# Cached keys of the paged attention turned ahead of time on VectorE and kept in DRAM, in place of TensorE transposes

## The reference

```python
q = rmsnorm(x @ Wq.T) ; k = rmsnorm(x @ Wk.T) ; v = x @ Wv.T   # 32, 8, 8 heads of 128
q, k = rope(q, pos), rope(k, pos)                    # pos = cache_seqlens + token
kc = k_cache[block_table].reshape(bsz, 512, 8, 128)  # 16 pages of 32 tokens
vc = v_cache[block_table].reshape(bsz, 512, 8, 128)
k_all, v_all = concat(kc, k), concat(vc, v)          # 640 keys
scores = where(valid, q . k_all * SCALE, -1e30)      # valid: token < cache_seqlens
o = softmax(scores) . v_all
attention2 = o.reshape(b, s, 32 * 128) @ Wo.T
x = x + attention_0(...) ; x = x + ffn_0(...)
x = x + attention_1(...) ; x = x + quantised_ffn(attention2)
```

## Time and profile before

| | us |
|---|---|
| median of 3 runs | 2040.61 (2037.54 to 2041.23) |
| the profiled execution, whole | 2036.61 |
| its span in the trace | 2034.7 |
| PE busy | 1986.8, 98% |
| DVE busy | 1534.6, 75% |
| ACT busy | 1324.8, 65% |
| POOL busy | 805.8, 40% |

### The profile page before, as it was taken

One profiled execution on the slowest core, in us unless ns is written; L12 is line 12 of the kernel. 1 busy time (PEld: TensorE's weight loads), 2 busy tenths in 40 slices (PEclk: granted clock), 3 DMA queues, 4 the chain that ended last, 5 costly groups with the idle time before them and its releaser, 6 DMA issues.

```text
span 2034.7 us, 35876 instructions
## 1 busy us (share of the span) xinstructions
PE 1986.8 (98%) x12477; PEld 1695.1 (83%) x12477; DVE 1534.6 (75%) x3383; ACT 1324.8 (65%) x3796; POOL 805.8 (40%) x797
## 2 busy tenths in 40 slices
PE   6999999999999999999999999999999999999997
PEld 5778677888888888888888888888888888888774
DVE  6777764556656555687887888878878888888998
ACT  4676763445554544576776777767767767777785
POOL 3200015100000000056666666666666666666662
PEclk9999999999999999999999999999999999999999
DMA  7301101101201110121111111211211111112010
GB/s 261 99 28 48 53 1 73 62 32 37 68 32 39 56 53 1 58 79 31 62 53 31 63 51 32 71 44 36 80 32 63 53 32 62 53 31 83 26 31 37
DMA packets 45011, 108.62 MB, mean 53 GB/s; under 512 B 15634, under 2 KB 21010, under 8 KB 40354
## 3 DMA queue, kind: packets, MB, share of 16 engines
q1 hardware_dynamic: 28450, 72.74, 10.3%
q0 software_dynamic: 16384, 33.59, 5.6%
HBM read 103.14 MB, written 3.15 MB: 52 GB/s over the span
## 4 chain that ended last, share of the span: by engine, by line
PE 91%; DVE 4%; ACT 3%; issue 1%; DMA 1%; SPq 0%; DVEq 0%; ACTq 0%
PE PS L1662 10%; PE PS L1487 9%; PE PS L1430 9%; PE PS L1566 9%; PE PS L1674 8%; PE PS L1629 7%; PE PS L1647 7%; PE PS L1580 4%; PE PS L1443 4%; PE PS L1632 3%; PE PS L342 3%; PE PS L1458 3%; PE PS L1473 2%; PE PS L498 1%; PE PS L1465 1%; PE PS L1598 1%
## 5 line engine op out<-in xcount | busy, mean ns | idle before, releaser
L2528 POOL DMA_INDIRECT kcache<-in_kcache,rows x256 | 249.6, 975 | 533.1 <-DVE x_res L1829 462.4
L2536 POOL DMA_INDIRECT vcache<-in_vcache,rows x256 | 257.2, 1005 | 124.2 <-issue 58.4
L2002 DVE CUSTOM_DVE_ANT_0 pr<-PS,ffn_weights,sm 128x640 f32<-128x640 f32 x256 | 224.6, 885 | 87.5 <-PE PS L1632 87.5
L2387 ACT ACTIVATE pr<-pr,sm 128x640 f32<-128x640 f32 x256 | 212.5, 830 | 40.1 <-DVE sm L2002 39.3
L2018 DVE TENSOR_TENSOR prT_lo<-PS,prT_hi 128x512 fp32r<-128x512 f32 x320 | 209.2, 686 | 37.0 <-ACT prT_hi L2398 30.8
L2398 ACT ACTIVATE prT_hi<-PS 128x512 fp32r<-128x512 f32 x320 | 178.0, 597 | 61.1 <-PE PS L1647 60.5
L1647 PE MATMUL PS<-consts,pr 128*128 128x128 f32 x1280 | 172.3, 273 | 2.2 <-DVE prT_lo L2018 1.7
L1647 PEld LDWEIGHTS PS<-consts,pr 128*128 128x128 f32 x1280 | 149.7, 141 | 26.3 <-DVE prT_lo L2018 2.7
L2542 POOL TENSOR_TENSOR vcached_lo<-vcache,vcached_hi 128x512 fp32r<-128x512 f32 x64 | 83.7, 1308 | 218.7 <-ACT vcached_hi L2370 218.7
L1629 PE MATMUL PS<-kT_hi,qT_hi 128*128 128x320 f32 x512 | 154.4, 309 | 2.5 <-DVE sm L2002 1.2
L1629 PE MATMUL PS<-kT_lo,qT_hi 128*128 128x320 f32 x512 | 154.1, 309 | 0.0
(11 more groups left out here) (321 smaller groups left out, 6178.1 us busy)
## 6 DMA issues: line engine op xcount, KB each, us to landing
arena<-in_wqkv SPq DMA_DIRECT2D x16, 1536.0 KB, 6.5
arena<-in_wo SPq DMA_DIRECT2D x16, 1024.0 KB, 5.4
arena<-in_wcT SPq DMA_DIRECT2D x8, 1024.0 KB, 6.7
kcache<-in_kcache,rows POOLq DMA_INDIRECT x256
vcache<-in_vcache,rows POOLq DMA_INDIRECT x256
arena<-in_xT SPq DMA_DIRECT2D x8, 256.0 KB, 7.8
x_res<-in_x SPq DMA_DIRECT2D x1, 2048.0 KB, 13.5
ffn_weights<-in_alibi SPq DMA_DIRECT2D x2, 1024.0 KB, 7.1
```

The source lines that it names most:

```text
L2002: dve.tensor_tensor_reduce(pr2[:, h, :].rearrange("p (a n) -> p a n", a=2), PS[:, SCORE_BANK[h]:SCORE_BANK[h] + 2, 0:HALF], keymask[:, b, ...
L2387: act.activation(pr2[:, h, :], pr2[:, h, :], ACT.Exp, bias=nm2[:, h:h + 1], scale=-1.0, accum_out=rs2[:, h:h + 1]).then_inc(a2_ex, 1)
L2528: pool.indirect_dma_start(out=kcache[:, c, :], out_offset=None, in_=T["kcache"], in_offset=bass.IndirectOffsetOnAxis(ap=rows[:, g, b, c:c ...
L2536: pool.indirect_dma_start(out=vcache[:, c, :], out_offset=None, in_=T["vcache"], in_offset=bass.IndirectOffsetOnAxis(ap=rows[:, g, b, c:c ...
```

## The change

- PE's turn_cached_k is gone. The keys are turned during attention 1 by DVE: POOL gathers the keys of item n (four gathers of 128 rows) in another order of rows into key_pages, DVE transposes them in blocks of 32x32 (turn_keys, one instruction of 128x512 float32), and POOL stores the result (256 KB, rows of 512 bytes) to a DRAM tensor turned_kept. The 64 turns are done at the end of DVE's step1(i) for i = 5 to 61: one in an item, two when i % 8 is 5.
- The row numbers of these gathers come from key_page_i, loaded at the start by four more transfers of SP. Each of them spreads 32 page numbers, which lie 4 elements apart in DRAM, over 32 partitions, so its elements are 4 bytes each.
- In attention 2 SP loads the turned keys of an item by four transfers of 64 KB into kcache; ACT's hi_of_cached_k and DVE's lo_of_cached_k read kcache instead of bank 3. SP waits for the last store before the first of these loads. The weight loads are put between them, at b = 2.
- pool_masks now waits for the last of the 64 stores, since the masks lie where the key buffers were. Then come load_values(0) and factors(0), as before. POOL issues no key loads in attention 2.
- project_out(i) goes to bank 3 (the last item's to bank 0) and waits for two of the four row maxima; the wait for add(i-1) in scores moves from head 0 to head 1.
- Order: DVE does lo_of_o(i-1) before the row maxima, reciprocals(2, 3) before normalise(1), lo_of_cached_k after add. ACT does normalise(2) and (3) before k_squares and hi_of_own_v, and hi_of_cached_k after hi_of_probs(1); for item 0 it stands in item 62 of attention 1, ahead of kT_copy1(63).

The diff, cut:

```diff
             for q in range(4):
                 sp.dma_start(page_i[q * 32:(q + 1) * 32, :], T["pages"][q, :].partition_broadcast(32)).then_inc(s_setup, 16)
+            for q in range(4):
+                sp.dma_start(key_page_i[q * 32:(q + 1) * 32, :],
+                             T["pages"].rearrange("c (b q) -> q (c b)", q=CHUNKS)[q, :].partition_broadcast(32),
+                             allow_slow_non_contiguous=True).then_inc(s_setup, 16)
...
+            dve.tensor_scalar(key_row0[:], key_page_i[:], float(PAGE * G), cst["inpage"],
+                              ALU.mult, ALU.add).then_inc(s_setup, 1)
...
+        key_pages = fw[:, B * D:B * D + 2 * CACHED].rearrange("p (s c d) -> p s c d", s=2, c=CHUNKS)
+        key_turned = fw[:, B * D + 2 * CACHED:B * D + 4 * CACHED].rearrange("p (s r c n) -> p s r c n", s=2, r=4, c=CHUNKS)
+        key_rows = area(28160, G * B * CHUNKS).bitcast(I32).rearrange("p (g c b) -> p g c b", g=G, c=CHUNKS)
+        turned_kept = nc.dram_tensor("turned_keys", [ITEMS, 4, P, P], F32).ap()
+        FIRST_TURN, LAST_TURN = GH + 1, ITEMS - 3
+
+        def turns_in(i):
+            if not FIRST_TURN <= i <= LAST_TURN:
+                return range(0)
+            first = i - FIRST_TURN + (i - FIRST_TURN + B - 1) // B
+            return range(first, min(first + 1 + (i % B == FIRST_TURN), ITEMS))
+
+        def pool_turned_keys(pool):
+            def gather(n):
+                g, b = group_of(n)
+                wait(pool, s_kpt, n - 1)
+                wait(pool, s_kpg, 16 * CHUNKS * n)
+                for c in range(CHUNKS):
+                    pool.indirect_dma_start(out=key_pages[:, n % 2, c, :], out_offset=None, in_=T["kcache"],
+                                            in_offset=bass.IndirectOffsetOnAxis(ap=key_rows[:, g, c, b:b + 1], axis=0)
+                                            ).then_inc(s_kpg, 16)
+
+            def store(n):
+                pool.wait_ge(s_kpt, n + 1)
+                wait(pool, s_kps, 16 * n)
+                pool.dma_start(turned_kept[n, :, :, :].rearrange("r p n -> p r n"),
+                               key_turned[:, n % 2, :, :, :].rearrange("p r c n -> p r (c n)")).then_inc(s_kps, 16)
+
+            pool.wait_ge(s_x2, B)
+            ch = Chain(pool, s_chp, counted["pool"])
+            ch.link(pool.tensor_tensor(key_rows.rearrange("p g c b -> p g (c b)"),
+                                       key_row0[:].unsqueeze(1).broadcast_to([P, G, B * CHUNKS]),
+                                       kvhead[:].unsqueeze(2).broadcast_to([P, G, B * CHUNKS]), ALU.add))
+            counted["pool"] = ch.n
+            gather(0)
+            gather(1)
+            for n in range(ITEMS):
+                store(n)
+                if n + 2 < ITEMS:
+                    gather(n + 2)
...
+            pool.wait_ge(s_kps, 16 * ITEMS)
...
+            def load_keys(n):
+                wait(sp, a2_kcl, n)
+                for r in range(4):
+                    sp.dma_start(kcache[32 * r:32 * (r + 1), :, :],
+                                 turned_kept[n, r, :, :].rearrange("(a j) n -> j a n", j=32)).then_inc(a2_kg, 16)
+
+            load_weights2(0)
+            sp.wait_ge(s_kps, 16 * ITEMS)
+            sp.wait_ge(s_wst, 16 * UNITS_Q)
+            for n in range(ITEMS):
+                load_keys(n)
+                g, b = group_of(n)
+                if b == 2 and g + 1 < G:
+                    load_weights2(g + 1)
+                elif b == 2:
+                    load_quantised()
...
-            def turn_cached_k(n):
-                pe.wait_ge(a2_kg, 16 * CHUNKS * (n + 1))
-                if n == 0:
-                    pe.wait_ge(a1_kTc, ITEMS)
-                for c in range(CHUNKS):
-                    mm = pe.transpose(bank(3, P, c * P), kcache[:, c, :], ident)
-                mm.then_inc(a2_kcT, 1)
...
                 for h in range(GH):
-                    if h == 0:
+                    if h == 0 and i == 0:
+                        pe.wait_ge(a1_max, ITEMS)
+                    if h == 1:
                         wait(pe, a2_acc, i - 1)
...
-                    pe.wait_ge(a2_max, 4 * (i + 1) + 4)
+                    pe.wait_ge(a2_max, 4 * (i + 1) + 2)
                 for h in range(GH):
                     for j, (a, c) in enumerate(PARTS):
-                        mm = pe.matmul(bank(0), o2[a][:, h, :], w_out[c][:, h, :],
+                        mm = pe.matmul(bank(OUT_BANK[i + 1 == ITEMS]), o2[a][:, h, :], w_out[c][:, h, :],
...
+                for n in turns_in(i):
+                    turn_keys(n)
...
-                dve.tensor_tensor(kT2[1][:, 0:CACHED], bank(3), kT2[0][:, 0:CACHED], ALU.subtract).then_inc(a2_kcl, 1)
+                dve.tensor_tensor(kT2[1][:, 0:CACHED], kcache[:].rearrange("p c d -> p (c d)"), kT2[0][:, 0:CACHED],
+                                  ALU.subtract).then_inc(a2_kcl, 1)
+
+            def turn_keys(n):
+                dve.wait_ge(s_kpg, 16 * CHUNKS * (n + 1))
+                wait(dve, s_kps, 16 * (n - 1))
+                dve.transpose(key_turned[:, n % 2, :, :, :].rearrange("p r c n -> p c r n"),
+                              key_pages[:, n % 2, :, :].rearrange("p c (r n) -> p c r n", r=4)).then_inc(s_kpt, 1)
...
+                if i:
+                    lo_of_o(i - 1)
                 for h in range(GH):
                     row_max(i, h)
-                if i:
-                    lo_of_o(i - 1)
                 reciprocals(i, (0, 1))
                 normalise(i, 0)
+                reciprocals(i, (2, 3))
...
                 if more:
                     lo_of_own_v(i + 1)
-                    lo_of_cached_k(i + 1)
                     norm_k(i + 1)
                 if q >= 4:
                     to_steps(q - 4, 1)
                 if i:
                     add(i - 1)
                 if more:
+                    lo_of_cached_k(i + 1)
                     lo_of_q(i + 1)
...
+                    hi_of_cached_k(0)
...
-                act.wait_ge(a2_kcT, n + 1)
-                act.activation(kT2[0][:, 0:CACHED], bank(3), ACT.Copy).then_inc(a2_kch, 1)
+                act.wait_ge(a2_kg, 16 * 4 * (n + 1))
+                wait(act, a2_sc, GH * n)
+                act.activation(kT2[0][:, 0:CACHED], kcache[:].rearrange("p c d -> p (c d)"), ACT.Copy).then_inc(a2_kch, 1)
...
+                normalise(i, 2)
+                normalise(i, 3)
                 if more:
                     k_squares(i + 1)
                     hi_of_own_v(i + 1)
-                normalise(i, 2)
-                normalise(i, 3)
                 if q >= 2:
                     scale_hidden(q - 2, 0)
-                if more:
-                    hi_of_cached_k(i + 1)
                 if i + ITEMS - FROM_X < B:
                     hi_of_x(i + ITEMS - FROM_X)
                 hi_of_probs(i, 0)
                 hi_of_probs(i, 1)
                 if more:
+                    hi_of_cached_k(i + 1)
                     hi_of_q(i + 1)
                 if new_out:
...
+            pool_turned_keys(pool)
             pool_masks(pool)
             pool_paged(pool)
```

More of the change, by code:

```diff
@@ L162, in build @@
         rows = sb("rows", [P, G, B, CHUNKS], I32)
+        key_page_i = sb("key_page_i", [P, B * CHUNKS], I32)
+        key_row0 = sb("key_row0", [P, CHUNKS * B], I32)
         clen_i, clen = sb("clen_i", [P, B], I32), sb("clen", [P, B])
@@ L278, in build @@
         s_ym, s_g8 = sem("token_means"), sem("gate_ready")
-        NLOADF, NSETUP = 6, 10
+        NLOADF, NSETUP = 6, 14
         SPLIT = (0, 0), (0, 1), (1, 0)
@@ L1178, in dve_positions @@
             dve.tensor_scalar(row0[:].rearrange("p b c -> p (b c)"), page_i[:], float(PAGE * G), cst["inpage"],
-                              ALU.mult, ALU.add).then_inc(s_row0, 1)
-            dve.tensor_copy(kvhead[:], cst["kvhead"]).then_inc(s_row0, 1)
+                              ALU.mult, ALU.add).then_inc(s_setup, 1)
+            dve.tensor_scalar(key_row0[:], key_page_i[:], float(PAGE * G), cst["inpage"],
+                              ALU.mult, ALU.add).then_inc(s_setup, 1)
+            dve.tensor_copy(kvhead[:], cst["kvhead"]).then_inc(s_setup, 1)
             ch.link(dve.tensor_copy(clen[:], clen_i[:]))
-            dve.tensor_scalar(pos[:], clen[:], cst["token"], None, ALU.add).then_inc(s_row0, 1)
+            dve.tensor_scalar(pos[:], clen[:], cst["token"], None, ALU.add).then_inc(s_setup, 1)
         def pool_tables(pool):
@@ L1249, in build @@
         SCORE_BANK = 0, 2, 4, 0
+        OUT_BANK = 3, 0
         QPARTS = KT + 1
@@ L1314, in table, with load_quantised @@
                              T["alibi"][:, h * P:(h + ALIBI_PART) * P]).then_inc(s_alibi, 16)
+            def load_quantised():
+                sp.wait_ge(a2_wl, QPARTS * G)
+                sp.wait_ge(s_wst, 16 * (UNITS_Q + 1))
+                sp.dma_start(wT16.rearrange("p w t n -> p (w t n)"),
+                             wT_kept.rearrange("p w t n -> p (w t n)")).then_inc(s_fi, 16)
```

(28 more changed lines are left out.)

28 lines of the change are left out of this document (4 added, 24 removed).

## The result

The changed kernel takes 2063.24 us (median of 4 runs, 2059.64 to 2065.74), the kernel before 2039.64 beside it: a ratio of 1.0115 with a 95% interval of 1.0097 to 1.0133, so 20 to 27 us slower. Forecast was no measurable change, 2039.4. The time lies outside the range of 2025 to 2056.

What follows compares the result with a forecast made beforehand. PE was taken to bound the kernel in attention 2. Terms -19.2 (attention 2), +14.5 (seam), +3 (start) and +0.5 (attention 1) sum to -1.2: 2035.4, or 2039.4 us on the median's scale, range 2025 to 2056.

Steps and rivals of the forecast that it cites:

- What bounds the kernel: Middle items of attention 2: PE busy throughout, 17.17 us an item; savings count until the next engine's chain is as long.
- the removed transposes: Attention 2: an item loses 0.45 us on PE, 28.8 us over 64 items if nothing else comes late.
- What becomes late in its place: Attention 2: DVE's later row maxima delay the third lo_of_probs; period 0.31 us shorter, taken as 0.29, 16.2 over 56 items.
- A: Whole kernel: the forecast itself, 2039.4 us, own range 2031 to 2047; chance 0.40.
- B: Attention 2: DVE catches up and the full 0.45 us an item is gained, -27.5 instead of -19.2, 2031; chance 0.22.
- The last items: End of attention 2, where PE isn't dense: 0.45 us an item comes through in part, a gain of 3 (0 to 5).
- Rival D: Attention 2: late row maxima stall PE in each item, period falls by only 0.1 us; +12, 2052; chance 0.17.
- The seam: Between the attentions: masks and factors(0) wait for the last store of turned keys, delaying norm_k(0); +14.5 us (10 to 20).
- The start: Start: four transfers of 1024 single elements take 4.0 us of all DMA engines, partly beside slack; +3 us (0 to 6.5).
- Attention 1: 64 turns of 0.69 us hidden in DVE's idle 1.53 us before its reciprocal; +0.5 us (0 to 3).
- rival C: Attention 1: POOL doesn't keep the pace, store issue 3.9 us, turns end some 70 us late; about 2110; chance 0.08.

Runs made afterwards that it cites:

- the store moved: Changed kernel with the page table loaded by one transfer and the store of 1024 scale factors moved behind the first load of turned keys: 2035.94 us, ratio 0.9990.
- the masks spread: Changed kernel with one page-table load, the scale-factor store moved later and the key masks written item by item instead of all eight first: 2026.58 us, ratio 0.9940.
- the single page load: Changed kernel with the keys' page table loaded by one transfer of 128 rows of 512 bytes, picked apart by four VectorE operations: 2041.72 us, ratio 1.0021.
- all four repairs: Changed kernel with one page-table load, scale-factor store moved later, masks written per item, first turned keys' high part in item 63: 2022.06 us, ratio 0.9924.
- the strided loads last: Changed kernel with its four strided page-table loads unchanged but issued behind all loads of layer 0: 2043.20 us, ratio 1.0031.
- o's low part late: Changed kernel with o's low part put back after the four row maxima: 2084.55 us, ratio 1.0232.
- the first experiment: Kernel before with only the four transfers of 1024 single elements added to the start, their data unused: 2055.13 us, ratio 1.0084.

## Why the prediction was wrong

**What bounds the kernel, and the removed transposes:** right. Projection and output product now lie as in the earlier trace rows: 0.24 between the product's first two matmuls, 0.45 less an item.

**What becomes late in its place:** wrong in size, and with it the choice between A and B. The first row maximum came at 1.44 (forecast 1.43). But I let the four follow each other at 0.88, as before. That pace was PE's: the kernel before fed them head by head, with 0.88 from head to head on PE's timeline:

```profile
1508.91 0.31 PE L1629 MATMUL PS<-kT_hi,qT_hi 128*128 128x320 f32 x1
...
1509.80 0.31 PE L1629 MATMUL PS<-kT_hi,qT_hi 128*128 128x320 f32 x1
```

Started behind PE, they run at 0.80 (1541.25 to 1543.66, three steps), so the fourth is 0.23 earlier. Another 0.2 was idle time that I took for DVE's work: before, DVE's first lo_of_probs started 0.42 behind the instruction ahead of it (1517.06 to 1517.48), after 0.21 (1548.80 to 1549.01). The third lo_of_probs starts at 1552.40 - 1539.81 = 12.59 and ends at 13.27, ahead of the 13.41 that PE asks for. DVE doesn't bind; the period is 16.72, that of rival B. A row of instructions that follow each other closely gives the pace of the chain, not that of the engine; the busy time of one (0.87 to 0.89 here, with 0.80 from start to start) doesn't give the engine's pace either, since it overlaps the next. The dense items gave 18.3 instead of 16.2, and not B's 25, because of the changes of group (0.63 us of each lost, seven times) and one of the two POOL stops (1.6), which no row of before showed.

**The last items:** -3 expected, +2.9 in this trace. From the 57th turn_k to the last, the kernel before takes 133.5 us, the changed one 136.4; the experiments with the store moved and with the masks spread take 135.9 and 135.8, those with the single page load, all four repairs, the strided loads last and o's low part late 134.4 to 134.5. The 1.5 us between the two sets lie in one item (20.5 to 20.6 us against 19.0 in the three of the second set that have the new order). PE waits some 1.75 us for a row maximum in it in both sets; then the granted clock falls in the first set (0.88 in 1918 to 1928 us of the changed kernel) and stays at 1.00 in the second. The second POOL stop with its 1.3 us is in all of them; without it and the clock the last items would be some 0.3 us under before. The row that I had, DVE busier than PE there, said that a saving on PE isn't worth anything; I took 3 of the 3.6 us (eight items of 0.45) all the same. Rival D's mechanism wasn't it, since the old order gave the same time.

**The seam:** right, 13.0 to 14.4 against 14.5, by the mechanism that was forecast. The last turn ended at 902.2, the store's issue took 0.79 (taken: 1.3), landing and start of the masks 2.05 more, the masks 19.9 (taken: 18.7), factors at 928.0; the small misses cancel. ACT's wait in item 62 was contained in it, as I had said: POOL's chain ran beside it without a wait for it. It came out as a cost of some 4 us only when the masks were spread, and then had to be repaired by itself.

**The start:** the failed step with the largest error, +18.6 against +3. I divided the work of a store of 1024 elements over all DMA engines, from the DMA shares of two stretches, and got 0.9 us. A share of the engines is no time when a transfer can't use them: the loads ran for some 15 us at a share of 0.11, which is 3.7 us for 1024 elements, and the load that PE needs stood behind all four. The row of that store could have warned me: 11.6 us to landing for 4 KB, where 256 KB need 2.0. It isn't the price either, which would be 46 us for four. It holds a weight load issued just ahead of it, at 758.42 on SP's queue, and some 6 us after the DMA share had fallen to 0.00 (from 764 us on), and the ordinary page_i loads at the start of the kernel before, also 4 KB, have 10.3 us to landing. The Trainium skill ("DMA: Bandwidth & Descriptors", Rules for kernel authors) says that a non-contiguous last dimension becomes one descriptor per element and should be rearranged to be contiguous; the page of the profile of the first experiment agrees: 19794 DMA packets under 512 B against 15634 before, 4160 more for 4096 elements. What they cost, 17 us against 2 for the same table in rows, is this case's own measurement.

**Attention 1:** the second failed step, +10.1 against +0.5. The turns fit into DVE's idle time as forecast (0.70 us each, POOL's store 0.80, the pace held; rival C didn't occur). What was missed is that a turn also waits for its transfers: 6.6 us where the store of scale factors, harmless before, got a waiter behind it, and 3.5 where weight loads share the engines.

**The rivals:** none had a price for loads that hold a queue, or for a turn that waits for its transfers. B had the period of the dense items right. D ended on the right side for a reason that the runs refute: PE wasn't held in each item.

## What to carry to other kernels

A transfer with elements of a few bytes isn't priced by its share of the DMA engines. Ask how long it keeps others waiting, on its own queue and on others; move it last or load rows and pick them apart on an engine. When work is moved so that new operations wait for transfers, old slow transfers that had no waiter must be priced again. A chain that runs back to back under a slower producer shows the producer's pace, and that is not what binds once it starts behind the producer. And a change that loses can hold a gain: the transposes off PE with o's low part first were worth 16 us once the start, one store, the masks and one early wait were put right.

## What the runs showed of the hardware

- 4096 single elements of 4 bytes keep a queue for some 15 us beyond the loads ahead of it, at a DMA share of 0.11 and 1 GB/s, in four transfers over 32 partitions as in one over 128; the next transfer's issue took up to 18.18 us. A store of 1024 such elements was followed by a store of 256 KB on another queue that needed some 11 us to land.
- The block transpose of 128x512 float32 on DVE takes 0.70 us, as an elementwise pass of that size (0.69).
- PE's granted clock was 0.50, the lower level of 1.2 GHz, in the stretch 30 to 35 us of the changed kernel, in which PE stood still, against 0.95 in the one before, in which it had worked for 1.32 us. After a wait of some 1.75 us in the last items it fell in three traces (to a mean of 0.88 in the changed kernel's stretch 1918 to 1928 us) and stayed at 1.00 in three others; a fall cost 1.5 us.
- POOL stood still for 3.3 to 3.5 us between two gathers twice in attention 2, in the changed kernel and in each of its six variants, always ahead of the 434th and the 547th of the 576 transfers that POOL issues, and never in the kernel before, whose POOL issues 512. Its cause wasn't tested and stays open.
